# Unread products ahead of each group of a node update's products

## The reference, cut to what matters

```python
h = relu(layernorm(x)); x = x + L0(h)   # relu(concat(h, mean of messages) @ W_upd + b_upd)
h = relu(layernorm(x)); x = x + L1(h)   # (weighted sum of neighbours + h) @ W.T + b
h = relu(layernorm(x)); x = x + L2(h)   # attention over edges, then two layer norms around
                                        # gelu(y @ W1 + b1) @ W2 + b2
h = relu(layernorm(x)); x = x + L3(h)   # exponential of a graph Laplacian, 80 sparse steps
```

## Time and profile before

| what | us |
|---|---|
| median of 3 runs | 5066.35 |
| span of the profiled execution (the only time it has) | 5595.3 |
| first node update | 1421 to 1741 |
| second node update | 2337 to 2590 |
| third node update | 3283 to 4120 |

### The profile page before, as it was taken

How to read it: one execution, slowest core, us unless ns; L and a number is a source line. 1 busy time by engine, 2 the same in 40 slices (tenths; PEclk the granted TensorE clock), 3 DMA queues, 4 the chain that set the end, 5 groups by cost and what they waited for, 6 DMA issues and landing times. The chain is left out here.

```text
span 5595.3 us, 57187 instructions
## 1 busy us (share of the span) xinstructions
PE 3211.8 (57%) x11864; PEld 1985.9 (35%) x11864; DVE 2682.7 (48%) x6366; ACT 1037.9 (19%) x1952; POOL 2831.6 (51%) x2538
## 2 busy tenths in 40 slices
PE   3554726555895268775666626777735545455534
PEld 1222515444674157552222214555522222222212
DVE  6877722111453022364666625777754444444423
ACT  0222411111221011121211102333311111111100
POOL 0364048886113850134666646777515555587741
PEclk7776655555555555555555555555557777776665
DMA  5222621111562110253111132443311111133214
GB/s 186 83 60 69 263 91 22 22 22 17 141 162 80 23 16 1 73 198 111 36 35 36 35 55 47 79 95 69 79 54 29 28 28 28 27 31 28 28 16 95
DMA packets 337013, 363.38 MB, mean 65 GB/s; under 512 B 236964, under 2 KB 268846, under 8 KB 336864
## 3 DMA queue, kind: packets, MB, share of 16 engines
q1 hardware_dynamic: 222752, 262.44, 14.4%
q0 software_dynamic: 94096, 80.75, 11.4%
q10 hardware_dynamic: 20016, 18.41, 1.0%
HBM read 188.07 MB, written 188.35 MB: 67 GB/s over the span
## 5 line engine op out<-in xcount | busy, mean ns | idle before, releaser
L843 PE MATMUL e_ps<-e_msg,e_hot 128*128 x2408 | 583.2, 424 | 540.0 <-issue 304.5
L843 PEld LDWEIGHTS e_ps<-e_msg,e_hot 128*128 128x128 f32 x2408 | 538.0, 327 | 631.3 <-issue 627.1
L1733 POOL DMA_INDIRECT u_a<-attended,dst_end x392 | 468.5, 1195 | 153.4 <-issue 115.5
L815 DVE TENSOR_TENSOR e_ps<-e_ps,e_before 128x65 f32<-128x65 f32 (+1 forms) x172 | 40.1, 233 | 991.9 <-PE e_ps L843 513.6
L2364 PE MATMUL d_pl<-d_hot,d_fields 128*65 128x512 f32 x712 | 498.2, 866 | 0.0
L2019 POOL DMA_INDIRECT list<-s_rec,s_place x200 | 201.5, 1008 | 316.6 <-DVE s_place L1935 258.0
L735 POOL DMA_INDIRECT e_msg<-from_src,e_src x200 | 205.6, 1028 | 288.2 <-DMA e_first<-lot_first 233.8
L2308 POOL DMA_INDIRECT flows<-d_out,d_end x160 | 263.4, 1646 | 106.6 <-issue 101.7
L2295 POOL DMA_INDIRECT d_near<-term,d_rec x196 | 190.8, 973 | 236.4 <-DMA d_rec<-list 181.5
L938 POOL DMA_INDIRECT a_ends<-h,a_src x200 | 197.6, 988 | 202.9 <-DMA a_etype<-in_etype 113.8
L2356 PE MATMUL d_pr<-ident,d_scan 65*128 65x65 f32 x356 | 63.6, 327 | 400.8 <-DVE d_scan L2474 341.1
(11 more groups left out here) (369 smaller groups left out, 7774.3 us busy)
## 6 DMA issues: line engine op xcount, KB each, us to landing
u_z<-h SPq DMA_DIRECT2D x28, 896.0 KB
x<-sums SPq DMA_DIRECT2D x28, 896.0 KB, 7.8
u_x<-x SPq DMA_DIRECT2D x28, 896.0 KB
terms<-s_zeros SPq DMA_DIRECT2D x16, 812.5 KB
s_key_row<-src_key SPq DMA_DIRECT2D x50, 256.0 KB
h1d<-u_h SPq DMA_DIRECT2D x14, 910.0 KB
u_z<-h1d SPq DMA_DIRECT2D x14, 910.0 KB
term<-u_h SPq DMA_DIRECT2D x14, 910.0 KB
```

Of the source, the lines that this page charges most:

```text
L843: last = nc.tensor.matmul(to, hot[s][:, q, :], rows, start=False, stop=q == LOT - 1)
L1733: pool.indirect_dma_start(A[s][:, j, :], None, net.attended[:, :], bass.IndirectOffsetOnAxis(ap=net.dst_end[:, tile:tile + 1], axis=0)).th ...
```

## The change

`set_bias` now begins with `fill`: 3 products in the first node update, 4 in the others, each of the 128 x 128 bf16 identity with the identity four times over, 512 columns. In the first two node updates they go to a PSUM bank of their own, `unread`, that nothing reads; in the third they go to the group's own bank `po`, which the bias product then overwrites. In the first two node updates PE also issues 4 such products ahead of its wait for each supertile's input, and 16 ahead of the first. Nothing else moves on any engine.

```diff
+        fillers = 3 if layer == 0 else 4
+        if layer < 2:
+            unread = ps("unread")
...
+                def fill(bank, times):
+
+                    for _ in range(times):
+                        nc.tensor.matmul(bank[:, :], net.identb[:, :], net.identb[:, :].unsqueeze(1).to_broadcast([P, 4, P]),
+                                         start=True, stop=True)
+
                 def set_bias(b, which):
-
+                    fill(unread if layer < 2 else po[b], fillers)
                     nc.tensor.matmul(po[b][:, 0:J * C], net.ones3[:, :],
                                      net.bias_parts[:, which, :, :].rearrange("k j c -> k (j c)"), start=True, stop=False)
...
                 if layer < 2:
                     def step(c, start=False):
+                        fill(unread, 16 if start else 4)
                         pe.wait_ge(z_ready, c[0] + 1)
                         products((Z if layer == 0 else A)[c[1]], (c[0], c[1]), start)
```

## The result

The changed kernel takes 5184.55 us (median of 4 runs, 5177.22 to 5188.44) against 5065.37 for the kernel before in the same series (4 runs, 5062.44 to 5067.75): a ratio of 1.0232, 95% interval 1.022 to 1.0245. It is slower by 119 us; 161 were forecast. The span of its profiled execution is 5182.8 us, so this trace stands for the timed runs. That of before (5595.3) does not: there the first two node updates last as in a second trace (experiment 1), but stages that the change doesn't touch are longer (the edge sums between the first and the second node update 567 us against 396 in the trace of after, the last stage, with the 80 sparse steps, 1434 against 1287).

A forecast was written before the change was run, and what follows sets the result against it. PE, mostly at 1.2 GHz, was taken to limit the first node update and part of `mlp`, with several engines taking turns in the second; 56 + 4 + 46 + 55 = 161 us, 5066 + 161 = 5227 us, range 5030 to 5390.

The forecast's parts named there:

- rival two: All three node updates: unread products do not lift the clock, or only for moments; +400 us, 5466 us; chance 0.17.
- rival one: All three node updates: clock held through the waits, high nearly throughout; together -48 us, 5018 us; chance 0.20.
- the signs named before: Trace after: clock 0.6 to 0.85, falling behind each wait for the square; stages about 380, 300 and 810 us.
- The price of a group: With unread products, low and high clock: first stage 4.34 and 2.32 us, second 3.59 and 1.91, `mlp` 5.71 and 3.07.
- One product: One unread product of 512 columns on PE costs 0.43 us at the low clock, 0.21 at the high.
- First stage: +56 forecast for the groups and +4 for the burst: First node update: +4.0 us per supertile, 56 us over 14; the 16 products at the start taken as 4 us.
- of the four groups behind it three low and one high: First stage, groups behind the wait for the square: 3 x 1.29 - 0.73 = +3.1 us per supertile.
- The low end of the forecast: Each wait costs one group only: +0.6, +2.1, +0.7 us per supertile by stage, +52 us in all, 5118 us.
- Second stage: +46 forecast: Second node update, per supertile: low group behind the wait +1.72, next +0.7, start +0.9; +3.3 us, burst hidden.
- Third stage: +55 forecast: Third node update, per supertile: `mlp` three low groups +5.2, two high -1.8, `attend` +0.5; +3.9 us.
- Its own products do not bring the clock back: First node update before the change: 305 us at 0.50 although PE was busy 281 of them.
- None of them runs in a wait of a group: Unread products stand behind a group's waits for ScalarE and VectorE; only the 4 or 16 at supertile starts precede a wait.

The follow-up runs named there:

- experiment 1: The kernel before run once more with no edit, for a second trace: 5516.25 us, ratio 0.9954 to the kernel before.
- Experiments 2 to 4: The change in the first, second or third node update alone, each against the kernel before: ratios 0.9981, 1.0041 and 1.026.
- long_waits: Kernel before plus, in the first node update only, 18 and 8 unread products in the waits and 4 at supertile starts: 5456.66 against 5524.31 us, ratio 0.9915.
- third_only: Kernel before plus the unread products in the third node update alone, 4 a group, no bursts: ratio 1.026.
- one_each: Kernel before plus one unread product ahead of each bias product in all three node updates, none at starts: ratio 1.0126.
- mlp_only: Kernel before plus 4 unread products ahead of each bias product of `mlp` in the third node update, nothing elsewhere: ratio 1.0211.
- waits_third: Kernel before plus 10, 8, 14 and 10 unread products ahead of four waits in the third node update only: ratio 1.0059.
- again_after: The changed kernel run once more, unedited, against the kernel before on the same chip: ratio 1.0297.

## Why the prediction was right

**The direction and the way there are shown for the first two stages.** The clock rises at a supertile's start, falls at the wait for the square and comes back some groups later, as the timelines in the section on the result show. With 0.83, 0.88 and 0.80 neither rival two (all below 0.55) nor rival one (the first above 0.95) holds. Experiments 2 to 4 show that each stage loses by itself. Of the signs named before, 0.88 lies above the 0.6 to 0.85 that were forecast, and the stages came to 337, 294.5 and 766 us for 380, 300 and 810. The total is nearer than its parts: the first stage was forecast 38 us too high, and the third agrees by luck.

**The price of a group** held: 2.34 high and 4.35 low for 2.32 and 4.34 in the first stage, 1.94 high for 1.91 in the second. One product is 0.22 us high (18 from 1590.20 to 1594.20 in long_waits), for the forecast 0.21. The Trainium skill ("TensorE: Matmul & The Clock Gate", section "Back-to-back issue gap") gives about 131 ns for a product of 512 columns in a sustained stream. The trace does not agree: the 18 in a row take 0.22 us each, and the measurement decides.

**First stage: +56 forecast for the groups and +4 for the burst; +17 and +5 measured** (320 to 337.3; the burst from 1371.93 to 1376.75 in the trace). The step that failed is "of the four groups behind it three low and one high": 22 low groups of 98 are 1.6 per supertile. A group that is high and not low saves 1.29 + 0.73 = 2.0 us, 1.4 of them 2.9: the forecast 320/14 + 4.0 = 26.9 us per supertile becomes 24.0, and 337.3/14 is 24.1. The one supertile with three low groups took 27.9 us. The wait did grow, 1.40 to 2.54 us, as it should with VectorE's chain as the limit; in the second stage, whose high group is no shorter than before, it grew from 3.13 to 3.28 only.

**The low end of the forecast** (+0.6, +2.1 and +0.7 per supertile) is given without working. From the same prices the first of them, with one low group and three high behind the wait, would be -0.4 + 1.29 - 3 x 0.73 + 1.3 = 0.0. Measured were (337.3 - 320)/14 = +1.2, with 1.6 low groups.

**Second stage: +46 forecast, +41.5 measured** (253 to 294.5). One group a supertile runs low behind the wait, as forecast (13 low groups in 14 supertiles); the next, for which the sum had +0.7, runs high at no gain. The burst was hidden: behind it PE waits 8.9 us more for its input.

**Third stage: +55 forecast; +54 worked out, not seen** (885 less the 831 above). That the two agree is luck as far as the traces tell. The sum had three low groups per supertile in `mlp`; of its 98 groups 26 run low, 1.9 per supertile, and those at its start, which the sum had low, run high. In `attend`, for which the sum had +0.5 in all, 22 of 98 run low, 1.6 per supertile. Where the kernel before takes 5440 to 5525 us the third stage lost 117 to 158 us, and there the forecast's working, which counts PE's time alone, does not hold: most of the loss is the remote wait (203.9 us for 40.6 in third_only), which no term of it has. Why that wait gets longer isn't shown.

**"Its own products do not bring the clock back"** held for the first stage of that trace, not in general. In the second stage of the same trace, three groups behind a wait of 17.6 us, the clock came up with no unread product in the kernel:

```profile
2342.00 0.39 PE L1331 MATMUL u_po<-bias_parts,ones 3*128 3x256 bf16 x1
...
2343.90 0.28 PE L1331 MATMUL u_po<-bias_parts,ones 3*128 3x256 bf16 x1
```

It stayed up for 10.3 us. Such stretches are short and irregular (9 high groups of 98 in that stage, none in the second stage of long_waits, which is the same), so the unread products still are what keeps the clock up in the other traces.

**Rival one's price was a matter of place.** Its price for the first stage was 18 us less, since it left three unread products in each group. With all groups high and the products in the waits instead it is 48 us less (350.3 to 302.6). That the waits have room for them was the idea that the prediction came past ("None of them runs in a wait of a group") and did not price.

**Whether the transposes count for the clock** stays open: no experiment changed them alone.

## What to carry to other kernels

In the first stage, unread products paid only inside the waits where PE stood idle: 11 us where they fell short of the waits' end, 48 where they reached it. In front of every group their price eats into what the clock gives: in the first stage 0.63 of 1.36 us, in the second 0.84 of 0.80, and each group that still runs low pays them twice over. Before adding them, work out a group at both clocks, with and without them: where the high group with them is no shorter than the low one without (1.94 against 1.87 us), only a loss is left. Too few can be worse than none or than enough: one per group cost 31 us in the first stage and left the clock at 0.54; three, with those at the starts, cost 22. And look at what else a stage waits for: in the third, filling the waits gave nothing (912 us for 898).

## What was not expected of the hardware

The same kernel takes 5065 us in the first series and 5440 to 5525 us in the later ones, on three chips. Whether the chip makes the difference isn't shown. The first two node updates do not feel it: 375 and 318 us in the changed kernel's first trace, 380 and 317 in its later one. The third does, 885 and 1015.

In the later traces VectorE stands up to 26.4 us at a time in the third node update, before a taking-out in `mlp`, on something that the trace puts on no instruction of the core. In all it is 40.6 us before. It is more with unread products, but it doesn't follow their number: 71.4 us with 196 of them in that stage (one_each), 125.9 with 392 (mlp_only), 88.8 with 588 (waits_third), 123.0 and 203.9 with 784 (again_after, third_only).
